# Projections of an attention layer: three single-pass f32r products in place of one fp32 product

## The reference

```python
t = _to_tokens(x)                                  # (4, 256, 192)
t = t + _L1_attn_ref(_ln_t(t), w_qkv, b_qkv, w_proj, b_proj)

def _L1_attn_ref(x, w_qkv, b_qkv, w_proj, b_proj): # N=256, D=192, H=12, HD=16
    qkv = x @ w_qkv + b_qkv
    q, k, v = ...                                  # per head, 16 wide
    attn = softmax(q @ k.T * HD ** -0.5)
    return (attn @ v) @ w_proj + b_proj
```

## Time and profile before

| | |
|---|---|
| time, median of 3 runs | 265.62 us (265.25 to 265.77) |
| the profiled execution | 265.49 us, its span 263.6 us |
| granted clock of PE, mean | 0.98 of full |
| busy: PE, PEld | 238.2 us (90%), 168.3 us |
| busy: DVE, ACT, POOL | 152.1, 116.1, 67.0 us |
| DMA | 25.97 MB, mean 99 GB/s |

### The profile page before, as it was taken

One profiled execution on the slowest core, in us unless ns is written; L12 is line 12 of the kernel. 1 busy time (PEld: TensorE's weight loads), 2 busy tenths in 40 slices (PEclk: granted clock), 3 DMA queues, 4 the chain that ended last, 5 costly groups with the idle time before them and its releaser, 6 DMA issues.

```text
span 263.6 us, 5914 instructions
## 1 busy us (share of the span) xinstructions
PE 238.2 (90%) x2063; PEld 168.3 (64%) x2063; DVE 152.1 (58%) x335; ACT 116.1 (44%) x198; POOL 67.0 (25%) x70
## 2 busy tenths in 40 slices
PE   2999988799999999794987899999999999999982
PEld 2989866557677577462886685545655655455871
DVE  0228567566666666676417845665655665556183
ACT  0352154344434444425234025665665765656403
POOL 8600031000000000000510343465555544562100
PEclk9999999999999999999799799999999999999997
DMA  8999998774000000004600011111121111120343
GB/s 182 252 248 279 365 363 248 237 217 146 4 0 2 0 2 2 0 2 129 230 32 0 0 29 33 33 57 45 49 59 47 45 45 60 45 43 31 103 156 119
DMA packets 23911, 25.97 MB, mean 99 GB/s; under 512 B 4944, under 2 KB 22578, under 8 KB 23890
## 3 DMA queue, kind: packets, MB, share of 16 engines
q1 hardware_dynamic: 19666, 20.30, 26.1%
q0 software_dynamic: 2400, 4.92, 6.1%
q10 hardware_dynamic: 1824, 0.47, 1.0%
HBM read 22.13 MB, written 3.54 MB: 97 GB/s over the span
## 4 chain that ended last, share of the span: by engine, by line
PE 80%; DVE 11%; ACT 4%; issue 2%; DMA 1%; POOL 1%; DVEq 0%
PE grid L1267 10%; PE grid L1082 9%; PE bank L1295 8%; PE bank L1030 7%; PE grid L1274 6%; PE grid L1159 5%; PE bank L1110 4%; PE bank L1283 4%; PE bank L1096 3%; PE grid L947 3%; DVE main L710 2%; PE bank L1042 2%; PE bank L995 2%; PE grid L1055 2%; PE bank L961 2%
## 5 line engine op out<-in xcount | busy, mean ns | idle before, releaser
L886 DVE COPY main<-main 128x1152 f32 x43 | 33.1, 771 | 16.9 <-issue 14.8
L710 DVE TENSOR_REDUCE main<-grid 128x4 f32<-128x1024 f32 x24 | 29.3, 1224 | 23.0 <-PE grid L1055 23.0
L602 ACT ACTIVATE main<-down_all 128x576 f32 x44 | 29.9, 684 | 27.8 <-PE bank L1295 24.8
L571 ACT ACTIVATE main<-grid 128x1024 f32<-128x1024 f32 x24 | 24.4, 1023 | 30.0 <-PE grid L1082 30.0
L1267 PE MATMUL grid<-main 128*64 128x384 f32 x168 | 31.2, 488 | 0.6 <-DVE main L870 0.6
L442 POOL DMA_INDIRECT main<-xhat_rows,main x22 | 24.6, 1120 | 17.8 <-PE bank L1255 12.2
...
L1082 PE MATMUL grid<-main 32*128 32x256 f32 x192 | 26.6, 400 | 1.2 <-ACT main L571 1.2
L432 POOL DMA_DIRECT2D xhat_rows<-main x8 | 4.5, 574 | 89.4 <-DVE main L699 89.4
L1055 PE MATMUL grid<-main 32*128 32x256 f32 x192 | 26.2, 400 | 0.8 <-ACT main L530 0.8
L1295 PEld LDWEIGHTS bank<-main 128*64 128x64 f32 x240 | 17.1, 136 | 12.9 <-ACT main L602 10.3
L1295 PE MATMUL bank<-main 128*64 128x192 f32 x240 | 23.9, 333 | 0.1
...
## 6 DMA issues: line engine op xcount, KB each, us to landing
...
```

The costliest lines, as they stand in the source:

```text
L571: act.activation(probs[:, quad % 2, 2 * (n % 2):2 * (n % 2) + 2, :, :].rearrange("p h k n -> p h (k n)"), grid[:, score_banks(n), :], ACT. ...
L602: act.activation(w_dn[:, p, h, :], dn_e(expert(t, h)), ACT.Copy).then_inc(S["w_dn_ready"], 1)
L710: vec.tensor_reduce(negmax[:, g % QUADS, :, col:col + 33:32].rearrange("p q h -> p h q"), grid[:, max_banks(n), :].rearrange("p h (q n) -> ...
L886: vec.tensor_copy(w_gu[:, p, h, :], gu_e(expert(t, h))).then_inc(S["w_gu_ready"], 1)
```

## The change

- Queries, keys and values are projected in f32r. Tokens and weights are each split into a part rounded to f32r and the rest: `xT[0]`, `xT[1]`, `w_qk[0]`, `w_qk[1]`, `w_v[0]`, `w_v[1]`. A product is three: high x high, high x low, low x high (`mm3`).
- The 192 features are taken as 128 + 64 rows. Queries: rows 0 to 127, then 128 to 191 on rows 64 to 127. Keys: features 64 to 191, then 0 to 63 on rows 0 to 63. The two 64-row products follow each other.
- Queries go to bank 4 and keys to bank 5, for every m. So `project_qk(m)` waits for the eviction of m-1 (and from m = 3 for the shift of m-2, which reads bank 5), and `maxima_rows` for the eviction of the latest projection.
- The bias of queries and keys (with the 1 of the 17th key column) is added at the eviction, which becomes two instructions of 256 columns, Identity with a bias per row; the queries' scale stands there too. The values' bias is multiplied once with the output weights (`out_bias`, 3 fp32 matmuls) and joins the output's bias, for which `tok_b` on POOL now waits.
- The rest of the tokens is formed by DVE (`xT_lows`) after ACT's copy, twice ahead of the statistics of half two and twice after the first maxima.
- Weights come by 6 DMAs and biases by 8 small ones, in place of 4; DVE splits the weights by 8 instructions in place of 4 that spread them. `x2T` of the experts, which shares memory with `xT`, gets its constant rows after the projections, by POOL.

```diff
@@ -173,14 +182,13 @@
...
-        xT = carve(B * 2 * N).rearrange("p (b k n) -> p b k n", b=B, k=2)
-        wqkv = carve(2 * WQ).rearrange("p (k n) -> p k n", k=2)
-        carve(128)
+        xT = [carve_r(B * 2 * N).rearrange("p (b k n) -> p b k n", b=B, k=2) for _ in range(2)]
...
+        v_bias_rows = o_sb[:, 0].rearrange("p j n -> p (j n)")[:, 0:QUADS * 128].rearrange("p (j n) -> p j n", j=QUADS)
...
@@ -188,13 +196,19 @@
...
+        qk_bias = sb("qk_bias", [128, 2 * QUADS])[:, :]
+        v_bias = sb("v_bias", [128, QUADS])[:, :]
...
-        wqk_raw = carve(2 * 2 * C).rearrange("p (k n) -> p k n", k=2)
-        xhat = carve(NT * C).rearrange("p (t c) -> p t c", t=NT)
-        carve(0, MAIN - 4 * C)
+        w_raw = carve(5 * C).rearrange("p (m n) -> p m n", m=5)
+        w_all = [carve_r(WQ) for _ in range(2)]
+        w_qk = [w[:, 0:3 * QK].rearrange("p (m n) -> p m n", m=3) for w in w_all]
+        w_v = [w[:, 3 * QK:].rearrange("p (m n) -> p m n", m=2) for w in w_all]
+        xhat = probs_flat[:, 0:NT * C].rearrange("p (t c) -> p t c", t=NT)
+        carve(0, MAIN - 5 * C)
+        bproj_all = carve(C)
...
-        def qk_bank(m):
-            return bank[5 if m == 1 else 4]
+        def qk_bank(part):
+            return bank[4 + part][:, 0:N]
@@ -351,11 +365,19 @@
...
-            sp.wait_ge(S["w_zeroed"], 4)
-            sp.dma_start(wqk_raw[0:CH, :, :], a["w_qkv"][:, 0:2 * C].rearrange("(k p) n -> p k n", k=2)).then_inc(S["ld_qkv"], 16)
-            sp.dma_start(wqk_raw[CH:CH + 1, 1, :], a["b_qkv"][0:2 * C].unsqueeze(0)).then_inc(S["ld_qkv"], 16)
-            sp.dma_start(wqkv[0:CH, :, QK:], a["w_qkv"][:, 2 * C:].rearrange("(k p) n -> p k n", k=2)).then_inc(S["ld_qkv"], 16)
-            sp.dma_start(wqkv[CH:CH + 1, 1, QK:], a["b_qkv"][2 * C:].unsqueeze(0)).then_inc(S["ld_qkv"], 16)
+            sp.wait_ge(S["w_zeroed"], 6)
+            for part, cols in ((0, slice(0, C)), (3, slice(2 * C, 3 * C))):
+                sp.dma_start(w_raw[:, part, :], a["w_qkv"][0:128, cols]).then_inc(S["ld_qkv"], 16)
+            sp.dma_start(w_raw[:, 1, :], a["w_qkv"][C - 128:C, C:2 * C]).then_inc(S["ld_qkv"], 16)
+            sp.dma_start(w_raw[64:128, 2, :], a["w_qkv"][128:C, 0:C]).then_inc(S["ld_qkv"], 16)
+            sp.dma_start(w_raw[0:64, 2, :], a["w_qkv"][0:C - 128, C:2 * C]).then_inc(S["ld_qkv"], 16)
+            sp.dma_start(w_raw[64:128, 4, :], a["w_qkv"][128:C, 2 * C:3 * C]).then_inc(S["ld_qkv"], 16)
+            with nc.allow_non_contiguous_dma(reason="a bias per row"):
+                for r in range(4):
+                    sp.dma_start(qk_bias[32 * r:32 * r + HD, :],
+                                 a["b_qkv"][0:2 * C].rearrange("(j r d) -> r d j", r=4, d=HD)[r]).then_inc(S["ld_qkv"], 16)
+                    sp.dma_start(v_bias[32 * r:32 * r + HD, :],
+                                 a["b_qkv"][2 * C:3 * C].rearrange("(j r d) -> r d j", r=4, d=HD)[r]).then_inc(S["ld_qkv"], 16)
...
@@ -409,24 +431,30 @@
...
-            nc.gpsimd.memset(wqkv, 0.0).then_inc(S["w_zeroed"], 1)
+            nc.gpsimd.memset(qk_bias, 0.0).then_inc(S["w_zeroed"], 1)
+            nc.gpsimd.memset(v_bias, 0.0).then_inc(S["w_zeroed"], 1)
+            nc.gpsimd.memset(w_raw[:, 4, :], 0.0).then_inc(S["w_zeroed"], 1)
...
-            pool.wait_ge(S["w_zeroed"], 3)
...
-            nc.gpsimd.memset(wqkv[CH:CH + 1, 1, QK // 2 + HD:QK:32], 1.0).then_inc(S["w_zeroed"], 1)
+            pool.wait_ge(S["w_zeroed"], 5)
...
-            pool.wait_ge(S["w_zeroed"], 5)
...
-            for i, (part, value) in enumerate(((xT[CH:, :, :, :], 0.0), (xT[CH:CH + 1, :, 1, :], 1.0), (negmax, 0.0), (v_sb, 1.0))):
+            pool.wait_ge(S["w_zeroed"], 6)
...
+            for i, (part, value) in enumerate(((w_qk[0].bitcast(F32), 0.0), (w_qk[1].bitcast(F32), 0.0), (negmax, 0.0), (v_sb, 1.0))):
...
+            pool.wait_ge(S["out_bias_ready"], 1)
...
             nc.gpsimd.tensor_tensor(tok_b[:, :, :], tok[:, :, :],
-                                    bproj[:, :].unsqueeze(1).broadcast_to([128, NT, C]), ALU.add).then_inc(S["tok_b_ready"], 1)
+                                    bproj_all[:, :].unsqueeze(1).broadcast_to([128, NT, C]), ALU.add).then_inc(S["tok_b_ready"], 1)
+            pool.wait_ge(S["v_done"], B)
+            pool.wait_ge(S["qk_done"], B * QUADS)
+            nc.gpsimd.memset(x2T[CH:, :, :, :], 0.0).then_inc(S["bias_zeroed"], 1)
+            pool.wait_ge(S["bias_zeroed"], BIAS_SET + 1)
+            nc.gpsimd.memset(x2T[CH:CH + 1, :, 1, :], 1.0).then_inc(S["bias_zeroed"], 1)
...
@@ -521,13 +549,16 @@
...
             def xT_rows(b):
                 act.wait_ge(S["xT_done"], b + 1)
-                act.activation(xT[0:CH, b, :, :], bank[4 + b][0:CH, :].rearrange("p (k n) -> p k n", k=2), ACT.Copy).then_inc(S["xT_ready"], 1)
+                act.activation(xT[0][:, b, :, :], bank[4 + b][:, :].rearrange("p (k n) -> p k n", k=2), ACT.Copy).then_inc(S["xT_ready"], 1)
...
             def queries_keys(m):
                 act.wait_ge(S["qk_done"], m + 1)
                 if m >= 2 * QUADS:
                     act.wait_ge(S["st_done"], 2 * (m - 2 * QUADS) + 2)
-                act.activation(qk_sb[:, m % (2 * QUADS)], qk_bank(m)[:, :].rearrange("p (m n) -> p m n", m=2), ACT.Copy).then_inc(S["qk_ready"], 1)
+                for part in range(2):
+                    j = part * QUADS + m % QUADS
+                    act.activation(qk_sb[:, m % (2 * QUADS), part], qk_bank(part), ACT.Identity, bias=qk_bias[:, j:j + 1],
+                                   scale=1.0 if part else SCALE).then_inc(S["qk_ready"], 1)
...
             def values(b):
                 if b == 0:
@@ -557,6 +588,7 @@
                 token_major(s)
             deviations(HALVES[1], "mv_ready", "std_ready")
             act.activation(warm, eps_col, ACT.Exp)
+            act.wait_ge(S["bias_ready"], 2)
             for m in range(2):
                 queries_keys(m)
             for b in range(2, B):
-            dve.wait_ge(S["ld_qkv"], 4 * 16)
-            for part, scale in ((0, SCALE), (1, 1.0)):
-                for k in range(2):
-                    rows = slice(0, CH + k)
-                    vec.tensor_scalar(wqkv[rows, k, part * QK // 2:(part + 1) * QK // 2].rearrange("p (h d) -> p h d", d=32)[:, :, 0:HD],
-                                      wqk_raw[rows, k, part * C:(part + 1) * C].rearrange("p (h d) -> p h d", d=HD), scale, None, ALU.mult).then_inc(S["w_spread"], 1)
+            dve.wait_ge(S["ld_qkv"], 14 * 16)
+            dve.wait_ge(S["bias_zeroed"], 2)
...
+            def slots(w):
+                return w.rearrange("p m (h d) -> p m h d", d=32)[:, :, :, 0:HD]
...
+            raw_qk = w_raw[:, 0:3, :].rearrange("p m (h d) -> p m h d", d=HD)
+            for m in range(3):
+                vec.tensor_copy(slots(w_qk[0])[:, m], raw_qk[:, m]).then_inc(S["w_spread"], 1)
+            vec.tensor_copy(w_v[0], w_raw[:, 3:5, :]).then_inc(S["w_spread"], 1)
+            dve.wait_ge(S["w_spread"], 4)
+            for m in range(3):
+                vec.scalar_tensor_tensor(slots(w_qk[1])[:, m], raw_qk[:, m], 1.0, slots(w_qk[0])[:, m].bitcast(F32), ALU.mult, ALU.subtract).then_inc(S["w_spread"], 1)
+            vec.scalar_tensor_tensor(w_v[1], w_raw[:, 3:5, :], 1.0, w_v[0].bitcast(F32), ALU.mult, ALU.subtract).then_inc(S["w_spread"], 1)
...
@@ -675,6 +715,10 @@
...
+            dve.wait_ge(S["ld_const"], 2 * 16)
+            vec.tensor_scalar(qk_bias[:, 0:QUADS], qk_bias[:, 0:QUADS], SCALE, None, ALU.mult).then_inc(S["bias_ready"], 1)
+            vec.tensor_scalar(qk_bias[:, QUADS:], qk_bias[:, QUADS:], one_row, None, ALU.add).then_inc(S["bias_ready"], 1)
+            vec.tensor_copy(v_bias_rows, v_bias.unsqueeze(2).broadcast_to([128, QUADS, 128])).then_inc(S["v_bias_ready"], 1)
...
+            def xT_lows(b):
+                dve.wait_ge(S["xT_ready"], b + 1)
+                vec.tensor_tensor(xT[1][:, b, :, :], bank[4 + b][:, :].rearrange("p (k n) -> p k n", k=2),
+                                  xT[0][:, b, :, :].bitcast(F32), ALU.subtract).then_inc(S["xT_low"], 1)
...
             def maxima(n):
...
@@ -744,8 +793,15 @@
...
                 if half == 0:
...
+                    for b in range(2):
+                        xT_lows(b)
+            dve.wait_ge(S["v_bias_done"], 1)
+            dve.wait_ge(S["ld_attn"], 8 * 16)
+            vec.tensor_tensor(bproj_all[:, :], bank[7][:, 0:C], bproj, ALU.add).then_inc(S["out_bias_ready"], 1)
             for n in range(2):
                 maxima(n)
+            for b in range(2, B):
+                xT_lows(b)
             shift_queries(0)
             maxima(2)
...
@@ -1009,43 +1065,63 @@
                 if b == 2:
                     pe.wait_ge(S["img_ready"], 4)
                 pe.wait_ge(S["xhat_ready"], 2 * b + 2)
+                if b == 3:
+                    pe.wait_ge(S["out_bias_ready"], 1)
                 for k in range(2):
                     for h in range(2):
```

(49 more changed lines are left out.)

20 lines of the change are left out of this document (14 added, 6 removed).

## The result

The changed kernel took **275.85 us** (median of 4 runs, 271.72 to 278.17) against 265.69 for the kernel before (265.25 to 266.63) on the same chip: ratio 1.0238 [1.0149, 1.0326] (the brackets are a 95% interval). Ratios leave out runs that took over 1.5% more than the fastest of their kernel, here 278.17 and 277.78. The changed kernel is slower; 261.6 was forecast, and the range ended at 267.5. The profiled execution took 278.17 us (span 276.3, mean granted clock 0.933) and is the longest of the four, whose clocks lie from 0.933 to 0.958; so its times at full clock are read apart from those at half.

A forecast was written before the change was run, and what follows sets the result against it. PE, busy 52.1 of 53.3 us in the projecting attention loop, was taken as the bound. From 265.49 us, 6.3 saved in the loop and 2.45 added ahead of it gave 261.6 us, range 259.8 to 267.5.

The forecast's parts named there:

- `project_v`: Values' projection on PE: 12 records at 0.092 us, 1.12 us for 1.50, 0.38 less each.
- `project_qk`: Query and key projection on PE: 9 slots of 0.12 plus 0.12, 1.20 us for 1.92, 0.72 less.
- the fall: Ahead of the loop, PE's 2.6 us idle halves the clock: 1.9 us more, 263.5 us, chance 0.3 within the forecast's case.
- its case: Fast f32r records, with or without the clock's fall and late weights: 259.8 to 265.0 us, chance 0.62.
- rival 1: f32r records stream each column in two cycles: projection 2.15 us, `project_v` 2.07, whole kernel 275.9, slower; chance 0.13.
- Rivals 2 and 3: 2: 192-wide values' products cost as fp32, 273.6 us, chance 0.07. 3: 64-row halves do not overlap, 265.6, chance 0.13.
- The circle over the shift: Plain loop gaps: scores, DVE reduction and shift, then projection form a circle, 5.62 us for 5.93, 0.31 less, three times.
- The gaps with `project_out`: Two loop gaps that also hold `project_out`: 0.72 us less each, 1.4 in all, from 7.47 before.
- Ahead of the loop at full clock: Stretch before the loop: the second projection waits for its eviction; first scores at 49.75 for 47.30, 2.45 us more.
- ACT's evictions: Each eviction becomes two biased instructions on ACT, 0.9 us for 0.6, barely covered between exponentials in the loop.
- `tok_b`: On POOL ahead of the loop, moved behind `out_bias_ready`: off the chain, costs nothing.
- weights: Ahead of the loop: DVE's split takes 2.9 us within 4.2 free; late biases could cost up to 1.3, taken as nothing.

The follow-up runs named there:

- changed_again: The changed kernel unaltered, run again on another chip beside the kernel before: 273.82 us, ratio 1.0275.
- clock_fill: The changed kernel plus five unused fp32 products in PE's idle time between the first two projections: 271.19 us, ratio 1.0182.
- own_banks_m1: The changed kernel with its second projection in banks 6 and 7, waiting for the release of `out_bias` instead of the first eviction: 273.94 us, ratio 1.027.
- v_rows128: The changed kernel with the values' second product on all 128 rows, over weights zero in the added 64: 268.27 us, ratio 1.0024.
- before_idle: The all-fp32 kernel before, with its second projection made to wait for the first eviction: 271.57 us, ratio 1.0145.
- values_order: The changed kernel with `project_v` products ordered 128, 64, 64, 128 rows, removing one passage between row forms: 269.3 us, one run.
- qk_padded: The changed kernel with query and key tails as zero-padded 128-row products sharing one bank, without the added waits: 268.46 us, ratio 1.0049.
- padded_shift_wait: The changed kernel with queries, keys and values on 128 rows, where of the dropped waits only `project_qk`'s for the shift returns: 264.73 us, one run.
- clock_fill_both: The changed kernel plus five unused fp32 products between the first two projections and five after the last `attend`: 267.47 us, ratio 1.0021.

## Why the prediction was wrong, step by step

**The steps that failed.** Two terms of the forecast's sum were too small, `project_v` (2.03 us for 1.12) and `project_qk` (1.45 for 1.20). With what they measured, the sum at full clock is 267.4 us and not 261.6: slower than before by 1.9 us, not faster by 3.9. And the granted clock, which the sum left at that of the kernel before, was lower in every run: 0.933 to 0.958. With it goes the larger part of the error, some 8.4 us from 267.4 to 275.85.

**The clock.** The prediction saw the idle (2.6 us from 38.7, measured 2.39), named the fall, and gave it a chance of 0.3 within its case and 1.9 us. The price was right for one fall: from the first projection to the first scores it is 15.0 us in the first profile and 16.2 in changed_again, with falls of 3.4 and 6.8 us, and 13.2 in clock_fill without one, so 1.7 and 3.0 us. The chance was too low. Of six profiles in which PE idles 1.9 to 2.6 us between the first two projections, five have a fall that starts at 39 to 42 us (this kernel twice, own_banks_m1, v_rows128, before_idle), and values_order has none; of the seven without that idle, none has one before 50 us. So the idle makes a fall there likely, at fp32 as well, and the fill takes it away; that it must follow is refuted. What the prediction left out are the falls elsewhere. With both places filled the median was 267.47 us, clocks 0.981 to 0.989; changed_again had 273.82, clocks 0.951; with the first alone filled it was 271.19 (three chips). By these medians the larger part of some 6 us is lost after attention. It stays open why falls after attention are longer in some profiles (clock 0.70 over 126 to 134 in changed_again, 0.79 in the kernel before), and why one comes between 50 and 62 us in some (this kernel's first profile, own_banks_m1, qk_padded). The kernel before has clocks down to 0.956 as well, without the idle.

**`project_v`: term mis-sized, 2.03 us for 1.12.** The count of 12 records was right. A record of 192 columns costs 0.11 and not 0.092, and each change between 128 and 64 rows adds some 0.2. The trace of before has no such change, but it has one of like kind. Behind the 32-column products of `attend`, the second record of its `project_v` starts 0.27 us after the first, for 0.16 later on. The prediction had one such step in `project_qk`, within its 0.12 to the next group, and none inside a group. By the Trainium skill ("TensorE: Matmul & The Clock Gate", the section on LDWEIGHTS) a weight load of 128 columns takes 107 ns, by which I had estimated 1.28 us in all; v_rows128's 0.11 per record fits it, and 192 and 256 columns (0.112, 0.117) lie closer together than their columns do. That the weight load is what sets the 0.11 is not shown. By chance 2.03 is also near the 2.07 that the prediction gave for two cycles per column; the steps of 0.11 rule that out. (A small slip: 12 x 0.092 is 1.10, not 1.12.) Three gaps: 1.33 us each more than forecast, 4.0, of which 0.91 is this term and 0.25 the next.

**`project_qk`: 1.45 for 1.20.** Full rate and the overlap of the halves held, so rival 1 is false, although its 275.9 is by chance the time measured: a record comes after 0.12 us, not 0.225. The Trainium skill's two bytes per lane and cycle ("SBUF — State Buffer", the section against a bandwidth pool) is given there for bf16, and as a limit for f32r it doesn't fit these rows: 256 columns of four bytes came every 0.12 us. Rivals 2 and 3 are false too. What was left out is again the passage between kinds of records, twice 0.1. Padded to 128 rows it takes 1.60: the short rows still pay by themselves, by 0.15.

**The circle over the shift: mechanism right.** 1.28 + 3.08 + 0.15 + 1.45 = 5.96, forecast 5.62, before 5.93; the difference is the projection and the semaphore. padded_shift_wait confirms the wait alone (0.5). The gaps with `project_out` are 6.98 (forecast 6.75). So the loop's eight gaps sum to 3 x 5.96 + 3 x 7.05 + 2 x 6.98 = 53.0 for 53.2, and with the last projection to −0.7 us instead of −6.3.

**Ahead of the loop at full clock: right.** +2.58 (clock_fill) for +2.45. ACT's evictions: 0.82 a pair (0.9). `tok_b`, weights (first clip at 20.55, 0.16 later than before) and the clearing of `x2T`: nothing, as said.

With these terms the forecast's own sum is 265.5 − 0.7 + 2.6 = 267.4, and clock_fill_both, at a nearly full clock, measured 267.47. So the mis-sized terms alone took the forecast from 3.9 us faster to 1.9 slower, which agrees with the 1.4 to 2.2 that clock_fill_both loses at a like clock. The rest goes with the lower clock. Not all of it is accounted for: without the fills the kernel lies 3.4 to 3.9 us over the kernel before at like clock, and the 1.2 to 1.7 above clock_fill_both's 2.2 stay open.
